# A decoder's cross attention: adding the output into the residual tile in place, three such tiles, and the store issued ahead of the loads

## The reference, cut to what matters

```python
def _L1_xattn_ref(q, k, v, gamma):
    N_HEAD = 8
    ...
    scale = 1.0 / jnp.sqrt(jnp.asarray(dq, dtype=q.dtype))
    qk = jnp.einsum('bhdq,bhdl->bhql', qh, kh) * scale
    sm = jax.nn.softmax(qk, axis=-1)
    ret = jnp.einsum('bhql,bhdl->bhdq', sm, vh)
    ret = ret.reshape(B, Dv, Lq)
    return gamma * ret
...
x = _layernorm(x + _L1_xattn_ref(x, ctx_2048, ctx_2048, L1_xattn_gamma), axis=-1)
```

## Time and profile before

| | |
|---|---|
| median of 3 executions | 2038.38 us |
| lowest, highest | 2033.85, 2040.03 us |
| span of the profiled execution | 2041.2 us |
| PE matmuls busy over the span | 1832.9 us (90%) |
| DVE, ACT, POOL busy | 1253.9 (61%), 918.1 (45%), 290.8 (14%) us |
| cross attention within the profiled span | about 1600 to 1952 us |

### The profile page before, as it was taken

One profiled execution on the slowest core, in us unless ns is written; L12 is line 12 of the kernel. 1 busy time (PEld: TensorE's weight loads), 2 busy tenths in 40 slices (PEclk: granted clock), 3 DMA queues, 4 the chain that ended last, 5 costly groups with the idle time before them and its releaser, 6 DMA issues. The chain is left out here.

```text
span 2041.2 us, 33020 instructions
## 1 busy us (share of the span) xinstructions
PE 1832.9 (90%) x12272; PEld 1493.2 (73%) x12272; DVE 1253.9 (61%) x2330; ACT 918.1 (45%) x2376; POOL 290.8 (14%) x347
## 2 busy tenths in 40 slices
PE   6979999999997889999999987899997698889966
PEld 5868999999885778888888885677775455555543
DVE  3446444444447656555654536788887587778847
ACT  2225333333334443333333214676666587778811
POOL 0000000000012111111111001333334112111001
PEclk9989999999999999999999998999997899899988
DMA  3022000000014221101110013000013575665134
GB/s 106 32 95 92 21 22 22 22 21 1 22 53 129 83 73 42 47 19 40 48 37 17 11 42 124 12 32 32 32 53 96 148 170 147 151 150 127 49 118 142
DMA packets 86253, 136.62 MB, mean 67 GB/s; under 512 B 9480, under 2 KB 25480, under 8 KB 86096
## 3 DMA queue, kind: packets, MB, share of 16 engines
q1 hardware_dynamic: 86096, 134.52, 23.2%
HBM read 79.88 MB, written 21.05 MB: 49 GB/s over the span
## 5 line engine op out<-in xcount | busy, mean ns | idle before, releaser
L2224 ACT ACTIVATE e_p<-e_s_ps,e_nb 128x512 f32<-128x512 f32 x256 | 175.1, 698 | 45.5 <-DVE e_nb L2270 43.7
L2270 DVE TENSOR_REDUCE e_nb<-e_s_ps 128x2 f32<-128x1024 f32 x128 | 155.8, 1218 | 51.2 <-PE e_s_ps L2346 50.5
L1710 ACT ACTIVATE p<-p,nb,rq 128x128 f32<-128x128 f32 (+1 forms) x256 | 136.9, 541 | 92.9 <-DVE nb L1811 92.9
L2356 PE MATMUL e_t_ps<-ident,e_p 128*128 128x128 f32 x1024 | 147.7, 283 | 21.2 <-DVE e_pT L2277 13.5
L894 PE MATMUL yp<-ccy,toep 128*128 128x288 f32 x600 | 159.1, 413 | 5.7 <-ACT ccy L876 3.6
L2356 PEld LDWEIGHTS e_t_ps<-ident,e_p 128*128 128x128 f32 x1024 | 120.1, 146 | 58.9 <-issue 49.6
L80 PE MATMUL q_ps<-a_xt_hi,wq_hi 128*128 128x256 f32 x512 | 151.3, 296 | 4.1 <-DVE wo_lo L112 4.1
L1231 DVE SCALAR_TENSOR_TENSOR hm<-gu_ps,us_col,sg 128x256 f32<-128x256 f32 x88 | 42.3, 481 | 177.4 <-ACT sg L1120 177.4
L82 PE MATMUL q_ps<-a_xt_hi,wq_lo 128*128 128x256 f32 x512 | 145.7, 285 | 0.0
L81 PE MATMUL q_ps<-a_xt_lo,wq_hi 128*128 128x256 f32 x512 | 145.4, 284 | 0.0
L527 ACT ACTIVATE ex<-ex 128x512 f32<-128x512 f32 x64 | 40.4, 632 | 213.1 <-DVE ex L590 213.1
(11 more groups left out here) (300 smaller groups left out, 5151.7 us busy)
## 6 DMA issues: line engine op xcount, KB each, us to landing
x_after<-n_r SPq DMA_DIRECT2D x24, 512.0 KB, 3.0
toep<-padded_kernels SPq DMA_DIRECT2D x32, 256.0 KB, 3.6
qs<-e_xh SPq DMA_DIRECT2D x64, 128.0 KB, 2.5
qs<-e_xl SPq DMA_DIRECT2D x64, 128.0 KB, 2.6
ks<-e_ch SPq DMA_DIRECT2D x64, 128.0 KB, 2.6
ks<-e_cl SPq DMA_DIRECT2D x64, 128.0 KB, 2.7
x<-x_after SPq DMA_DIRECT2D x12, 512.0 KB, 4.5
x<-in_x SPq DMA_DIRECT2D x8, 512.0 KB, 4.0
```

Of the source, the lines that this page charges most:

```text
L1710: act.activation(p[n % 3][:, h, part[t]], p[n % 3][:, h, part[t]], ACT.Exp, bias=nb[i][:, t, h:h + 1], scale=rq[u][:, t:t + 1], accum_out= ...
L2224: act.activation(pr[i][:, a, :], s_ps[i][:, a, :], ACT.Exp, bias=nb[i][:, a:a + 1], accum_out=sums[t][:, j, q:q + 1]).then_inc(e_done, 1)
L2270: dve.tensor_reduce(nb[i][:], s_ps[i][:], AX.X, ALU.max, negate=True).then_inc(nb_done, 1)
L2356: last = pe.transpose(t_ps[a][:, k, :], pr[m % 2][:, a, k * P:(k + 1) * P], core.ident[:])
```

## The change

The output is added into the residual tile itself, `xr[b % 3]`, and statistics, normalising and store work on that tile. The norm of this phase has no tile `r` of its own any more (`own=False`), and there are three tiles `xr` in place of two, so the memory taken is the same. DVE no longer waits for a store; the wait is now in SP's program, before the residual of batch b is loaded into the tile: batch b-3 must have been stored from it. In SP's body the order is now stack(b+1), residual(b+1), store(b-1), loads of b+3, where it was stack, loads, residual, store.

```diff
-    def __init__(self, core, ctx, name, dst):
+    def __init__(self, core, ctx, name, dst, own=True):
...
-        self.r = sb("r", [P, T, D])
+        self.r = sb("r", [P, T, D]) if own else None
...
-        norm = Norm(core, ctx, "n5", y)
+        norm = Norm(core, ctx, "n5", y, own=False)
         xs = [core.x0, sb("e_x1", [P, T, D])]
-        xr = [sb(f"e_xr{u}", [P, T, D]) for u in range(2)]
+        xr = [sb(f"e_xr{i}", [P, T, D]) for i in range(3)]
...
-        r_loaded, o_scaled = [s("r_loaded0"), s("r_loaded1")], s("o_scaled")
+        r_loaded, o_scaled = [s(f"r_loaded{i}") for i in range(3)], s("o_scaled")
...
-                def residual(b, u):
-                    wait_from(sp, o_done, T * (b - 1))
-                    sp.dma_start(xr[u][:], rows(x, b)).then_inc(r_loaded[u], 16)
+                def residual(b):
+                    if b >= 3:
+                        sp.wait_ge(norm.stored, 16 * (b - 2))
+                    sp.dma_start(xr[b % 3][:], rows(x, b)).then_inc(r_loaded[b % 3], 16)
...
                 def body(b, u, more):
                     if not (ints(b) and b == B - 1):
                         stack(b + 1, 1 - u)
+                        residual(b + 1)
+                    if not (ints(b) and b == 0):
+                        norm.store(sp, b - 1, r=xr[(b - 1) % 3])
                     if more:
                         sp.wait_ge(c_turned, 2 * b + 4)
                         load(b + 3, 1 - u)
-                    if not (ints(b) and b == B - 1):
-                        residual(b + 1, 1 - u)
-                    if not (ints(b) and b == 0):
-                        norm.store(sp, b - 1)
...
                     dve.wait_ge(o_scaled, T * b + t + 1)
+                    r = xr[b % 3]
                     if t == 0:
-                        in_buffer(dve, r_loaded, b, u)
-                        norm.wait_stored(dve, b)
-                    dve.tensor_tensor(norm.r[:, t, :], xr[u][:, t, :], rb[:], ALU.add).then_inc(o_done, 1)
+                        dve.wait_ge(r_loaded[b % 3], 16 * (b // 3 + 1))
+                    dve.tensor_tensor(r[:, t, :], r[:, t, :], rb[:], ALU.add).then_inc(o_done, 1)
```

More of the change, by code:

```diff
@@ L2151, in stack @@
                                              src[j * CX:(j + 1) * CX, :, :].bitcast(F32)).then_inc(stacked[j], 16)
-                def residual(b, u):
-                    wait_from(sp, o_done, T * (b - 1))
-                    sp.dma_start(xr[u][:], rows(x, b)).then_inc(r_loaded[u], 16)
+                def residual(b):
+                    if b >= 3:
+                        sp.wait_ge(norm.stored, 16 * (b - 2))
+                    sp.dma_start(xr[b % 3][:], rows(x, b)).then_inc(r_loaded[b % 3], 16)
                 load(1, 1)
-                residual(0, 0)
+                residual(0)
                 sp.wait_ge(c_turned, 2)
@@ L2174, in _ @@
                 after.load_x(sp)
-                norm.store(sp, B - 1)
+                norm.store(sp, B - 1, r=xr[(B - 1) % 3])
                 sp.wait_ge(norm.stored, 16 * B)
@@ L2289, in scale_out @@
                     dve.wait_ge(o_scaled, T * b + t + 1)
+                    r = xr[b % 3]
                     if t == 0:
-                        in_buffer(dve, r_loaded, b, u)
-                        norm.wait_stored(dve, b)
-                    dve.tensor_tensor(norm.r[:, t, :], xr[u][:, t, :], rb[:], ALU.add).then_inc(o_done, 1)
+                        dve.wait_ge(r_loaded[b % 3], 16 * (b // 3 + 1))
+                    dve.tensor_tensor(r[:, t, :], r[:, t, :], rb[:], ALU.add).then_inc(o_done, 1)
                 def finish(b, u):
-                    norm.statistics(dve, b, [(o_done, T * b + t + 1) for t in range(T)])
+                    norm.statistics(dve, b, [(o_done, T * b + t + 1) for t in range(T)], r=xr[b % 3])
                 def body(b, u, first, last):
@@ L2309, in body @@
                         if m == HALF + 4 and not first:
-                            norm.apply(dve, b - 1)
+                            norm.apply(dve, b - 1, r=xr[(b - 1) % 3])
                 def tail(b, u):
```

## The result

The changed kernel takes 2019.38 us (median of 4 executions, 2018.70 to 2022.66), against 2038.86 for the kernel before (4 executions, the three shown above and one more). The medians are 19.5 us apart, against a forecast of 21.1. The estimated ratio is 0.9909 (the quotient of the two medians is 0.9905), with a 95% interval from 0.9893 to 0.9924, that is, 15.5 to 21.8 us less. A later group of runs on one chip gave a ratio of 0.9916 (0.9898 to 0.9933), with 2018.58 us against 2037.66. The profiled execution has a span of 2020.8 us and a time of 2022.66, so some 1.9 us lie around the span; the sum of the prediction had 2020.1 for the span.

A forecast was written before the change was run, and what follows sets the result against it. In cross attention, DVE's wait for a late store and PE's low clock after it lengthened four stretches; 11.0 us of wait plus 10.1 of clock, 21.1 less, took the median 2038.38 to 2017.3 us, range 2011 to 2028.

The forecast's parts named there:

- the sum of the prediction: Cross attention: four long stretches, 177.50 us, become four of 39.10 (156.40), 21.1 us less; 2020.1 for the profiled span.
- The reading by stretches: Cross attention cut at seven step-1 L2288 marks: four stretches of 44.35 to 44.40 us, two of 40.05 and 39.10.
- The control: Last bodies, turn near 1862: store issued early lands long before the turn; stretch of 39.10 us, clock 1.00.
- the turn near 1645: Start of the first stretch (40.05 us): no store waited for, L2293 held behind `e_cl`; nothing was to change.
- the hold: At the turns, POOL's subtraction `e_cl` keeps DVE's addition L2293 from ending, 1.63 us against 0.69; expected to stay.
- The two terms: At the four long turns: DVE's wait on the store, 11.0 us in all, and PE's low clock, 10.1 us.
- SP's order: SP's moved residual, store and loads were to cost nothing, with 4.4 us of cover for the loads.
- the check of the residual: Before the turn near 1685: residual issued before 1673, in place by 1682, so it would not be late.
- The port: Rival: at the turns `e_xl` goes ahead of the waiting L2293; stretches stay 44.4 us, 2038.4 us, no change; chance 0.04.
- The clock that doesn't return: Rival: PE's clock stays low after the turns; gain of 11.0 us only, 2027.4 us; chance 0.05.
- More than forecast: Rival: the 0.94 us collision of L2293 with POOL's subtraction also goes at four turns; 2013.5 us; chance 0.02.
- Slower by a low clock in a long busy stretch: Rival: PE, busy through six bodies without rest, gets its low clock midway; 2052 us if half of five bodies; chance 0.01.

## Why the prediction was right, point by point

**What bounds the phase.** The reading by stretches held. The control, the one body without loads, gave the length of five of the six stretches after: 39.10 against 39.09 to 39.12.

**The sum.** From the first to the last of the seven marks the kernel before took 256.65 us and the changed one 235.00: 21.65 less. Of this 21.1 is the four stretches (177.50 against 156.42), as forecast. Another 0.56 comes from the stretch at the turn near 1645 (40.05 to 39.49), which the prediction had left at nothing. It isn't the change's: L2293's length at that turn was 2.59 us before and 2.03 after, and 2.35 in the repeated run of the changed kernel, 2.85 and 2.87 with the tiles alone and the order alone. `e_cl` hangs there on the landing of the first stack, because ACT's rounding of the context waits for that: 0.86 us in the kernel before, 0.28 in the changed one, 0.62 in the repeated run. The prediction subtracted the 0.96 us by which L2293 was longer there (40.05 minus 0.96 is 39.09), as if the hold cost them. PE's rows of the kernel before, near 1645 and near 1685, say otherwise:

```profile
1645.48 1.07 PE L2356 MATMUL e_t_ps<-ident,e_p 128*128 128x128 f32 x8 [1.48 <-ACT e_pT L2232]
1648.00 1.06 PE L2380 MATMUL e_v_ps<-e_pT,e_vt 128*32 128x512 f32 x8 [0.44 <-DVE n_r L2293]
1684.57 1.06 PE L2356 MATMUL e_t_ps<-ident,e_p 128*128 128x128 f32 x8 [0.52 <-ACT e_pT L2232]
```

PE waited no longer for L2293 than at a freed turn; the 0.96 us lie in its wait for ACT's copy L2232 behind the late rounding, 1.48 against 0.52. In the changed kernel that wait was 0.91 us near 1645, 0.39 more than at its next turn, and the stretch is 0.39 us longer. The subtraction came out right because L2293's length and PE's wait grow by the same late rounding: the result was sound, its ground wasn't.

**From the marks to the span.** The span fell by 20.4, not 21.65, because the first mark came 1.47 us later (1646.07 against 1644.60) and the rest behind the last mark took 0.22 us less. In the repeated run the first mark came at 1640.72. The phases before it do the same work in each, so several microseconds in a comparison of two executions are theirs. The measured 19.5 and 19.1 us lie within that of 21.1, though the interval of the second, 13.7 to 20.8 us, ends just short of it; why the medians show a little less than the stretches stays open. The forecast time of 2017.3 us lies 2.1 below the measured one, and 0.5 of that is the kernel before, whose median came out higher with its fourth execution. The forecast of one time was closer than the executions of one kernel are to each other (2033.85 to 2040.03 for the kernel before), and to that extent lucky; what was forecast to a few hundredths is the stretches.

**The two terms.** 11.0 of wait and 10.1 of clock: the run with PE kept busy took back 10.05 in its four stretches with DVE's wait in place, and the 41.86 us that are left are 2.76 above 39.10, the share of the wait.

**SP's order.** "Nothing" was right. But the check of the residual rested on a wrong picture: the prediction had it in place "before 1685.28", as if that turn needed it. The residual loaded in body b is that of batch b+1, and is added in body b+2, a whole body later. In the run with the tiles alone it was issued at 1678.58, without effect. The reading of the rest of the order held: the loads were issued at 1678.90, when `c_turned` came, 4.4 us behind the store.

**What gave the gain.** The prediction took the two halves as one: the wait goes and the store comes early. Each is enough alone, and it should have said so; the earlier trace rows already show the wait in place and harmless behind an early store.

**The rivals.** The port: told apart above, it didn't take the wait's place at any turn, even with the two subtractions back to back. The clock that doesn't return: clock 1.00 in all stretches. More than forecast: the prediction priced the hold at 0.94 us a turn, as if DVE's delay were the stretch's. PE's idle time behind the hold is only 0.45 us, and moving the roundings so that the hold went brought 0.19. Slower by a low clock in a long busy stretch: 235 us at 1.00.

## What to carry to other kernels

Where one wait repeats at the turns of a loop, look for a turn of the same loop that escapes it, at the start or the end; its whole stretch, not the length of the wait, is the price: here the four waits were 1.7 to 3.8 us long, and all four stretches were 5.3 us too long, since a stretch also holds what POOL's subtraction and PE's clock add. A store that a later instruction must have seen land belongs on its queue where its data is ready, ahead of loads that nobody needs soon: here that did as much as a third buffer. And the length of a hold on one engine is not its price: here DVE was held for 0.94 us and the busiest engine stood idle for 0.45 of them, and taking the hold away by moving another engine's work cost most of that again elsewhere.

## What the runs showed of the hardware that I had not expected

- A DVE addition that waited behind a POOL subtraction got in ahead of the next one, which followed with no gap; that one lasted 2.83 us in place of 2.4.
- Repeating matmuls that change nothing made the kernel faster: 384 more of them, and 10.05 us less in four stretches, because PE worked through a DVE wait of 3.3 us and its clock stayed at 1.00.
- PE's idle times of 0.45 and 0.52 us in one turn left its clock at 1.00; after one of 2.46 us its matmuls ran at low clock, as after the 3.25 us of the kernel before.
- Transfers of 512 KB issued together land late: behind two loads and a residual, all issued within 2.5 us, the stores took 7.4 to 8.5 us in the kernel before and 7.5 to 9.0 with the tiles alone; issued ahead of the loads they took 3.2 to 4.9 us in the changed kernel and 3.1 to 5.5 with the order alone.
